# A whitening kernel: TensorE's phases of six rounds, each of two covariance pieces, two products and four steps of the chain

## The reference, cut to what matters

```python
x1 = x.reshape(N, C // G, G, H, W).transpose(0, 2, 1, 3, 4).reshape(N, G, -1)
xc = x1 - x1.mean(-1, keepdims=True)
cov = xc @ xc.transpose(0, 2, 1) / M + EPS * jnp.eye(G, dtype=x.dtype)
normA = jnp.linalg.norm(A.reshape(B, -1), axis=1)[:, None, None]
Y = A / normA
for _ in range(num_iters):
    T = 0.5 * (3.0 * I - Z @ Y)
    Y = Y @ T
    Z = T @ Z
decorr = Z / jnp.sqrt(normA)
y = weight1 @ decorr @ xc + bias1
```

## Time and profile before

| what | value |
|---|---|
| median of 3 runs | 498.11 us |
| the three runs | 498.11, 497.77, 507.7 us |
| span of the profiled execution | 506.6 us |
| its own time | not listed; the nearest run is 507.7 us |
| mean granted TensorE clock | 0.899 of 2.4 GHz |
| busy share of the span | TensorE 89%, VectorE 65%, ScalarE 68%, GpSimd 11% |
| moved | 75.51 MB in, 75.50 MB out |

### The profile page before, as it was taken

One profiled execution on the slowest core, in us unless ns is written; L12 is line 12 of the kernel. 1 busy time (PEld: TensorE's weight loads), 2 busy tenths in 40 slices (PEclk: granted clock), 3 DMA queues, 4 the chain that ended last, 5 costly groups with the idle time before them and its releaser, 6 DMA issues.

```text
span 506.6 us, 17928 instructions
## 1 busy us (share of the span) xinstructions
PE 450.2 (89%) x7872; PEld 285.0 (56%) x7872; DVE 329.5 (65%) x1043; ACT 342.5 (68%) x450; POOL 56.6 (11%) x108
## 2 busy tenths in 40 slices
PE   3678899999999999999999999999999999888800
PEld 3667766666566666666656666666666556423200
DVE  6886567777877787877777877777777765321000
ACT  5674478887777787877778878888787744433800
POOL 0000001111111111111110111111111111110410
PEclk9795579999999999999999999999999989855855
DMA  8999707999899999999999999999998545635890
GB/s 344 371 420 423 314 3 226 345 361 353 315 340 340 351 337 360 374 380 365 323 363 363 341 376 349 372 340 347 379 361 270 178 153 172 187 119 141 265 285 11
DMA packets 19774, 152.17 MB, mean 300 GB/s; under 512 B 3056, under 2 KB 3056, under 8 KB 3696
## 3 DMA queue, kind: packets, MB, share of 16 engines
q0 software_dynamic: 9952, 75.50, 41.8%
q1 hardware_dynamic: 9744, 75.52, 40.7%
HBM read 75.51 MB, written 75.50 MB: 298 GB/s over the span
## 4 chain that ended last, share of the span: by engine, by line
PE 85%; DMA 2%; ACT 2%; DVE 2%; issue 2%; POOL 1%; SPq 1%; DVEq 0%; POOLq 0%
PE cov_ps L591 32%; PE y_ps L606 32%; PE chain_ps L566 6%; PE chain_ps L562 5%; DMA b_col<-bias 2%; PE shift_ps L525 2%; PE chain_ps L572 2%; ACT image L310 1%; PE chain_ps L541 1%; POOL y L272 1%; PE chain_ps L551 1%; PE chain_ps L574 1%; PE chain_ps L560 1%; PE chain_ps L564 1%; PE chain_ps L558 1%
## 5 line engine op out<-in xcount | busy, mean ns | idle before, releaser
L319 ACT ACTIVATE image<-y_ps,y_bias 128x768 f32<-128x768 f32 x192 | 172.2, 899 | 103.4 <-PE y_ps L606 91.8
L403 DVE STREAM_TRANSPOSE transposed<-image 128x384 f32<-128x384 f32 x384 | 213.5, 571 | 13.0 <-issue 2.0
L591 PE MATMUL cov_ps<-transposed 128*64 128x65 f32 x4608 | 188.4, 235 | 9.6 <-DVE transposed L403 7.3
L606 PE MATMUL y_ps<-image,apply_w 64*64 64x384 f32 x1536 | 180.5, 542 | 1.4 <-ACT image L319 0.9
L591 PEld LDWEIGHTS cov_ps<-transposed 128*64 128x64 f32 x4608 | 161.6, 146 | 18.5 <-issue 11.6
L310 ACT ACTIVATE image<-image,shift 128x1152 f32<-128x1152 f32 x128 | 158.1, 1246 | 1.5 <-DMA image<-x 0.5
L562 PEld LDWEIGHTS chain_ps<-yz 32*32 32x32 f32 x576 | 20.9, 106 | 91.7 <-DVE yz L455 54.2
L270 POOL DMA_DIRECT2D y<-image x34 | 19.4, 570 | 425.9 <-ACT image L319 425.9
L455 DVE COPY yz<-chain_ps 64x64 f32<-64x64 f32 x144 | 29.6, 206 | 45.2 <-PE chain_ps L566 39.2
L606 PEld LDWEIGHTS y_ps<-image,apply_w 64*64 64x64 f32 x1536 | 42.4, 138 | 24.5 <-ACT image L319 9.0
L451 DVE SCALAR_TENSOR_TENSOR t_mat<-chain_ps,eye 64x32 f32<-64x32 f32 x144 | 25.0, 174 | 30.3 <-PE chain_ps L562 28.6
(11 more groups left out here) (61 smaller groups left out, 155.6 us busy)
## 6 DMA issues: line engine op xcount, KB each, us to landing
image<-x SPq DMA_DIRECT2D x63, 1152.0 KB, 10.1
y<-image POOLq DMA_DIRECT2D x31, 1152.0 KB, 9.8
y<-image POOLq DMA_DIRECT2D x62, 576.0 KB, 11.0
image<-x SPq DMA_DIRECT2D x2, 576.0 KB, 4.2
y<-image POOLq DMA_DIRECT2D x3, 384.0 KB, 11.6
y<-image POOLq DMA_DIRECT2D x6, 192.0 KB, 11.3
w_nat<-weight SPq DMA_DIRECT2D x4, 4.0 KB, 10.4
b_col<-bias SPq DMA_DIRECT2D x4, 0.1 KB, 10.7
```

What stands on the lines that cost most here:

```text
L319: nc.scalar.activation(xs[slot_of(c, i)][:, :, STRIP * q:STRIP * (q + 1)], y_ps[:, q % 2, :, 0:STRIP], ACT.Identity, bias=y_bias[:, c % 2, ...
L403: nc.vector.transpose(dst, xs[slot_of(c, i)][:, h, of_half:of_half + PIECE // 2]).then_inc(transposed, 1)
L591: ins = nc.tensor.matmul(cov_ps[rows, i, 0:GRAM], xt[q][:, t, 0:WIDE * G], xt[q][:, t, 0:GRAM], start=q == 0 and t < columns, stop=q == IM ...
L606: ins = nc.tensor.matmul(y_ps[out_rows, q % 2, h, 0:STRIP], apply_w[rows, c % 2, i].rearrange("p k g -> p (k g)"), xs[slot_of(c, i)][rows, ...
```

## The change

TensorE's phase becomes six rounds. A round is two covariance pieces of pair c with a chain step of pair c-1 between, then a step, an output piece of pair c-2, a step, an output piece and a step: four places a round, 24 a phase. The chain keeps Z and T of a pair as 64 x 64 block-diagonal matrices, so that a step is one matmul for both images; the step between the covariance pieces runs over all 128 rows, of which the upper 64 are zero. An update now adds 1.5 times the old matrix on VectorE, where T held that term before. The shift product is done in two matmuls of 64 columns. The gather has a PSUM place of its own.

Loads come in quarters (half a row of a half image). GpSimd centres the second quarter of each image, six images ahead of the one whose stores it has just issued; ScalarE centres three. VectorE makes its constants ahead of the first transposes. The small loads of weight and bias go through ScalarE's queue.

```diff
-PLACES = [1, 2] + list(range(4, STEPS + 2))
-STEP_AT = {place: t for t, place in enumerate(PLACES)}
-BULK = works("", "T1.0", "T1.1", "", "T1.2", "T1.3 T1.4",
...
+POOL_QUARTER = 1
+ACT_QUARTERS = [p for p in range(QUARTERS) if p != POOL_QUARTER]
+ROUNDS, SLOTS_A_ROUND = 6, 4
+AHEAD = 3 * PAIR
+STEP_AT = {1: NORM, 3: NEXT_0} | {t + 1: t for t in range(NEXT_0 + 1, SPREAD + 1)}
...
         def _(sp):
+            for n in range(IMAGES):
+                for p in range(QUARTERS):
+                    h, o = p // ROW_PARTS, p % ROW_PARTS
+                    if n >= SLOTS and o == 0:
+                        sp.wait_ge(stored[n % SLOTS][h], 16 * (1 + h) * (n // SLOTS))
+                    sp.dma_start(quarter_of(n, p), x_v[n, :, h, QUARTER * o:QUARTER * (o + 1)]).then_inc(
+                        loaded[n % SLOTS][p], 16)
...
         def _(pool):
+            def centre(n):
+                part = quarter_of(n, POOL_QUARTER)
+                pool.wait_ge(shift_copied, n + 1)
+                pool.wait_ge(loaded[n % SLOTS][POOL_QUARTER], 16 * (n // SLOTS) + 16)
+                nc.gpsimd.tensor_scalar(part, part, shift[:, n % 2:n % 2 + 1], None, ALU.add).then_inc(pool_centred, 1)
...
+            for n in range(AHEAD):
+                centre(n)
             for n in range(IMAGES):
...
                     store(n, slice(0, IMAGE_PIECES))
+                if n + AHEAD < IMAGES:
+                    centre(n + AHEAD)
...
         def _(act):
+            for c in range(PAIRS + 3):
+                for j in range(ROUNDS):
+                    before, f = (c - 2, 2 * j - 1) if j else (c - 3, FLAT - 1)
+                    if exists(before):
+                        output(before, f)
+                    if j == 1 and exists(c - 1):
+                        half_root(c - 1)
+                    n = PAIR * c + 1 + j // 3
+                    if n < IMAGES:
+                        if j % 3 == 0:
+                            copy_shift(n)
+                        centre(n, j % 3)
+                    if j == 0 and exists(c - 1):
+                        root(c - 1)
+                    if exists(c - 2):
+                        output(c - 2, 2 * j)
+                    if j % 3 == 2 and n + 1 < IMAGES:
+                        sum_shift(n + 1)
...
         def _(dve):
...
                 elif t == NORM:
-                    link(nc.vector.tensor_scalar(yz[:, 0, :], cov[:], HALF_RN, 2.0, ALU.mult, ALU.mult))
-                    link(nc.vector.scalar_tensor_tensor(
-                        out=yz[:, 1, :], in0=yz[:, 0, :], scalar=-0.5, in1=eye15[:], op0=ALU.mult, op1=ALU.add))
+                    link(nc.vector.tensor_scalar(y, cov[:], HALF_RN, 2.0, ALU.mult, ALU.mult))
+                    link(nc.vector.scalar_tensor_tensor(
+                        out=factor, in0=y.unsqueeze(1).to_broadcast([Q, PAIR, G]), scalar=-0.5, in1=own,
+                        op0=ALU.mult, op1=ALU.mult))
+                    link(nc.vector.tensor_tensor(z, factor.rearrange("p m g -> p (m g)"), eye15[:], ALU.add))
...
                 elif t < FOLD and (t - NEXT_0) % 2 == 1:
-                    link(nc.vector.scalar_tensor_tensor(out=t_mat[:], in0=product, scalar=-0.5, in1=eye15[:],
-                                                        op0=ALU.mult, op1=ALU.add))
+                    link(nc.vector.scalar_tensor_tensor(
+                        out=factor, in0=product.unsqueeze(1).to_broadcast([Q, PAIR, G]), scalar=-0.5, in1=own,
+                        op0=ALU.mult, op1=ALU.mult))
                 elif t < FOLD:
-                    link(nc.vector.tensor_copy(yz[:, first:2], following[:, first:2]))
+                    link(nc.vector.scalar_tensor_tensor(out=yz[0:Q, first:YZ], in0=yz[0:Q, first:YZ], scalar=1.5,
+                                                        in1=following[:, first:YZ], op0=ALU.mult, op1=ALU.add))
...
+            for c in range(PAIRS + 2):
+                for s in range(ROUNDS * SLOTS_A_ROUND):
+                    j = s // SLOTS_A_ROUND
+                    if s in STEP_AT and exists(c - 1):
+                        chain(c - 1, STEP_AT[s])
+                    if s == 9 and exists(c):
+                        covariance_out(PAIR * c)
+                    if s == 21 and exists(c):
+                        covariance_out(PAIR * c + 1)
+                    if s == 23 and exists(c):
+                        chain(c, GATHER)
+                    n = PAIR * c + (j + 2) // 3
+                    if n < IMAGES:
+                        transpose(n, (4 * j + 8) % TWELFTHS + s % SLOTS_A_ROUND)
...
         def _(pe):
+            for c in range(PAIRS + 2):
+                for j in range(ROUNDS):
+                    s = SLOTS_A_ROUND * j
+                    if exists(c):
+                        covariance(PAIR * c + 2 * j // IMAGE_PIECES, 2 * j % IMAGE_PIECES)
+                    if s in STEP_AT and exists(c - 1):
+                        chain(c - 1, STEP_AT[s], slice(0, P) if exists(c) else slice(0, Q))
+                    ahead = PAIR * c + 1 + j // 3
+                    if j % 3 == 0 and 1 < ahead < IMAGES:
+                        shift_of(ahead)
+                    if exists(c):
+                        covariance(PAIR * c + (2 * j + 1) // IMAGE_PIECES, (2 * j + 1) % IMAGE_PIECES)
+                    for m in range(1, SLOTS_A_ROUND):
+                        if s + m in STEP_AT and exists(c - 1):
+                            chain(c - 1, STEP_AT[s + m], slice(0, Q))
+                        if m < 3 and exists(c - 2):
+                            output(c - 2, 2 * j + m - 1)
+                if exists(c):
+                    gather(c)
```

More of the change, by code:

```diff
@@ L40 @@
 SLOTS = 10
-PERIOD = SLOTS // PAIR
 Q = PAIR * G
+HALF = P // 2
 SHIFT_PIXELS = PIXELS // 8
@@ new lines, in _ @@
+            sum_shift(0)
+            copy_shift(0)
+            for k in range(len(ACT_QUARTERS)):
+                centre(0, k)
+            sum_shift(1)
+            for c in range(PAIRS + 3):
[16 more added lines that the diff above has]
+                        sum_shift(n + 1)
@@ L481, in chain @@
                     link(nc.vector.tensor_tensor(RSQ, QUOTIENT, HALF_ROOT, ALU.add))
-            def phase(r, c):
-                for f, m, t, pair in places(r, c):
-                    if t is not None:
-                        chain(r, pair, t)
-                    for kind, n, *what in BULK[2 * f + m]:
-                        target = later(c, 0, n)
-                        if not exists(r, target[0]):
-                            continue
-                        if kind == "E":
-                            covariance_out(r, *target)
-                        else:
-                            transpose(r, *target, *what)
@@ L515, in _ @@
-            phases(dve, phase)
+            for k in range(8):
+                transpose(0, k)
+            dve.wait_ge(consts_in, 16 * (PAIR + BLOCKS))
+            nc.vector.transpose(w_t[:], w_nat[:]).then_inc(consts_ready, 1)
+            for c in range(PAIRS + 2):
[12 more added lines that the diff above has]
+                        transpose(n, (4 * j + 8) % TWELFTHS + s % SLOTS_A_ROUND)
@@ L610, in phase @@
-            def phase(r, c):
-                for f, m, t, pair in places(r, c):
-                    i, q = f // IMAGE_PIECES, f % IMAGE_PIECES
-                    if m == 0 and exists(r, c):
-                        covariance(r, c, i, q)
-                    if m == 0 and filling(r, c) and (c, f) in FILL_SHIFT:
-                        shift_of(0, FILL_SHIFT[c, f] // PAIR, FILL_SHIFT[c, f] % PAIR)
-                    done = output_at(c, f)
-                    if m == 1 and exists(r, done[0]):
-                        output(r, *done)
-                    if (c, f, m) == (1, 0, 0):
-                        pe.wait_ge(consts_ready, 1)
-                    if t is not None:
-                        chain(r, pair, t)
-                    ahead = later(c, i, 2)
-                    if m == 1 and q == SHIFT_AT and exists(r, ahead[0]) and not filling(r, c):
-                        shift_of(r, *ahead)
@@ new lines, in output @@
+            def output(c, f):
+                i, q = f // IMAGE_PIECES, f % IMAGE_PIECES
+                n, m = PAIR * c + i, FLAT * c + f
+                if f == 0:
+                    pe.wait_ge(chain_dve, OPS_TOTAL * (c + 1))
+                if m >= 2:
+                    pe.wait_ge(y_read, m - 1)
+                for row in range(2):
+                    for half in range(2):
+                        rows, out_rows = slice(HALF * row, HALF * (row + 1)), slice(HALF * half, HALF * (half + 1))
+                        h = row ^ half
+                        ins = nc.tensor.matmul(y_ps[out_rows, f % 2, h, 0:STRIP], apply_w[rows, c % 2, i].rearrange("p k g -> p (k g)"),
+                                               xs[n % SLOTS][rows, h, STRIP * q:STRIP * (q + 1)], start=True, stop=True)
+                ins.then_inc(y_done, 1)
```

474 lines of the change are left out of this document (189 added, 285 removed).

## The result

The changed kernel takes 535.91 us (median of four runs, 533.28 to 537.32); the kernel before takes 501.48 beside it. The ratio is 1.070, with an interval of 1.060 to 1.080. The forecast was 468 us, with a range up to 491: it had the wrong sign. The trace of the kernel before is of a slow execution (a span of 506.6 us, where three of the four runs beside it took 497.8 to 504.9), so a difference taken from two traces can be some microseconds larger than one between medians.

A forecast was written before the change was run, and what follows sets the result against it. TensorE was taken to set the pace. Fourteen phases shorter by 1.7 us save 24 us, filling 4, the second phase 1 and draining 1: 498.1 - 30 = 468 us, own range 454 to 481, overall range 450 to 491.

The forecast's parts named there:

- One row is missing here: GpSimd and VectorE working at once: if they exclude each other at the norm, TensorE waits 1.0 to 1.3 us more.
- the price of GpSimd's centring: GpSimd's centring of 1152 columns takes 2.5 us, an upper estimate from a 128x128 operation, and stays hidden.
- the norm is held by the centring: Rival: GpSimd's centring holds the norm's VectorE operations, 1.2 us a phase over 14 phases, giving 485 us; chance 0.22.
- None of the long chain operations reads two SBUF tensors: Argument against the held-norm rival, about VectorE's chain operations; that rival had 1.2 us a phase and chance 0.22.
- The centring is too slow: Rival: GpSimd takes 4.5 us, holds the norm 3.2 us and comes at the edge of its cover, 519 us; chance 0.07.
- The chain of items on TensorE: TensorE's covariance, chain, shift, output and gather items, priced start to start, account for the phase of 26.95 us.
- the forecast's own mechanism: TensorE sets the pace; less work there outweighs new lateness, so a phase falls 1.7 us to 25.25 us; chance 0.52.
- the work taken from TensorE: Per phase on TensorE: covariance 0.72, chain 2.4 and shift 0.38 us saved, 3.5 us in all.
- The 1.8 us of lateness: Per phase: TensorE's waits at the norm and following product, 1.3 us, and VectorE late in four places, 0.5 us.
- behind the last gather: Draining: the last chain phase, at clock 0.50, is bound by the same hand-overs and changes by -1 us.
- the transfers bind: Rival: DMA transfers set the phase; if rows of half the length cost 5%, 26.7 us a phase, 484 us; chance 0.06.
- VectorE becomes the bound: Rival: hand-overs or wider operations cost 0.04 us more each, adding 1.7 us a phase, giving 492 us; chance 0.10.

The follow-up runs named there:

- the first experiment: The changed kernel with ScalarE centring all four quarters and GpSimd none, the rest of the change kept: 447.73 us, ratio 0.888 to the kernel before.
- the kernel with both moves: The changed kernel with root operations three steps earlier and GpSimd's centring of odd images held until the norm's VectorE operations are done: 450.66 us.
- the small tile shape: The first experiment's kernel with the chain step between the two covariance pieces reading 64 rows in place of 128: 469.38 us, ratio 0.940.

## Why the prediction was wrong

**The step that failed** is the paragraph that begins "One row is missing here", with the price of GpSimd's centring above it. The mechanism was named there and made a rival, "the norm is held by the centring", at 485 us. Three things in its price were too small.

- The duration. 2.5 us was called an upper estimate, worked out from a 128x128 operation. Measured: 3.2 us, 2.8 ns a column against 2.2. A small operation of another kind was no upper end, and the estimate of about 1 us that stands beside it is further off still.
- The number of places. The text looked only at the norm, with 1.0 to 1.3 us. The rescale takes 1.9 us more than its 0.23, as a mean of sixteen. The addition of 64x1 in the second half of the phase, under the other image's centring, takes 2.3 us more than its 0.15, and was not looked for. "None of the long chain operations reads two SBUF tensors" was true and beside the point: one small operation on the chain's path is enough. The kernel in which ScalarE centres everything, and that in which GpSimd keeps clear of both, show that these two places make the whole loss.
- What follows a gap. The prediction priced a wait at its length. In the kernel after a steady phase is 30.7 us, in the first experiment 23.17: 7.5 us. TensorE's two waits account for 4.5 of these (2.47 and 2.81 us, against 0.24 and 0.52 in a phase of the first experiment). The rest is the clock. At about the end of each wait a stretch at 1.2 GHz begins, in which TensorE works nearly all the time, as these windows of the kernel after show (columns of the earlier trace rows):

```profile
255.90:259.30 3.40, 3.40 (x25) 1.71 (x22) 1.97 (x5) 0.90 (x1) 0.00 (x0) 0.51 0.84 231
269.60:273.00 3.40, 3.14 (x52) 3.08 (x52) 2.90 (x8) 1.35 (x2) 0.00 (x0) 0.50 1.02 236
```

TensorE's 6.5 us of work in them would take half as long at full clock, so they cost 3.3 us more. Waits and clock make 7.8, for the 7.5 measured; this is worked out from the traces, and no run changed the clock alone.

"The centring is too slow" had the right sign but another mechanism: it needed 4.5 us (3.9 ns a column, where its text says 3.5) and a late quarter. At 3.2 us GpSimd is in time: in the kernel with both moves VectorE waits 0.9 us in all for its quarters.

**What was right.** The chain of items on TensorE: the pair with its step takes 1.66 us (forecast about 1.6), a shift product 0.12 (from its first weight load at 264.46 to the next piece's at 264.58 in the kernel after), the first gather comes at 25.6 (forecast near 25). Freed of the centring, the forecast's own mechanism shows: phases of 23.1 to 23.2 us wherever TensorE does not pause.

**What was too cautious.** Of the work taken from TensorE, 3.5 us were forecast. Mean phases fell from 27.2 to 24.1 us, 3.1 (intervals between gathers, before and first experiment). The 1.8 us of lateness set against it are mostly not there: in the first experiment TensorE waits 0.52 and 0.24 us for the norm, not 1.3, and VectorE at 43.78 of 50 us does not yet bind: of the 1.6 us that the small tile shape added on TensorE, 1.2 reached the phase. So the rest of the change is worth 56 us, not 30. Between the traces of the kernel before and of the first experiment lie 61.9 us (between the medians 56): 3.1 up to the first gather (forecast 4), 5.2 in the second phase (forecast 1), 40.7 in the 14 phases behind it (forecast 24) and 12.9 behind the last gather (69.5 against 56.6; forecast 1). In proportion that last term was the most mis-sized. The chain phase that stands there ran at a clock of 0.50 before and runs at full clock in the first experiment:

```profile
388.00:421.50 33.50, 23.68 (x262) 9.69 (x260) 8.30 (x39) 21.06 (x27) 10.90 (x20) 1.00 0.84 257
```

The old order with GpSimd's centring has 68.3 us behind the last gather, and every kernel with the new order 55 to 58, so the gain belongs to the new order; which part of it brings it, no experiment took apart.

The rival "the transfers bind" expected shorter rows to cost; they gain 12. "VectorE becomes the bound" did not come about.

The version to keep is the first experiment's, 447.73 us, 11% below the kernel before, or that with both moves, 450.66, which the runs do not tell from it.

## What to carry to other kernels

Before work goes to an idle GpSimd, list every VectorE operation that can fall under it, the tiny ones too. Those with two tensors in SBUF, or a rescale from SBUF to SBUF, are held until the GpSimd instruction ends, and if TensorE hangs on one of them, the hold is paid in full and, as here, its clock falls as well. If GpSimd must be used, cut its work into short instructions, move the exposed operations away, or rewrite them with a scalar operand. A PSUM source may serve too: such operations ran free here, though no run rewrote a held one that way.

## What the runs showed of the hardware that was not expected

- Under an uncut centring a hold ends within 0.04 us (rescale) or 0.23 us (two tensors in SBUF) of the centring's recorded end, and it does not depend on how much the held operation does: an addition of 64 numbers took 2.3 us longer on average.
- GpSimd's tensor-scalar takes 3.2 us for 1152 columns of 128 partitions in float32, and 1.0 us for 288: about 0.27 us for each instruction and 2.55 ns a column, from these two.
- GpSimd is not slowed by VectorE's transposes: 3.2 us for a quarter in every kernel that leaves it whole, with and without holds.
- Loads of 576 KB in place of 1152 KB, with rows of half the length, gained 12 us of 460, most of it in the middle of the run, where TensorE's pauses end 0.9 to 1.6 us after a packet of instructions has come in.
